# A graph aggregation inside a fused block: boundary chunks gathered once for two groups, and groups dealt anew over the stages

## The chip, the cores and the metric

The kernel runs on one NeuronCore of a Trainium2 chip. Its engines work side by side, each through its own queue in order, and wait for one another by semaphores: TensorE (PE, matmuls; its weight loads are listed apart as PEld), VectorE (DVE), ScalarE (ACT), GpSimd (POOL, which here issues the gathers) and SyncE (SP, which issues the other transfers). The metric is the device time of one execution in microseconds (us). Time before: a median of 1892.01 us of three runs (1885.59 to 1893.51).

## The reference, cut to what matters

A block over 6250 rows of 512: a layer norm, then a graph branch and an attention branch added to x, and a feed-forward branch at the end. The part that the change touches is the graph branch's sum over 100,000 edges:

```python
h = jax.nn.relu(x @ W1 + b1) @ W2 + b2
row, col = (edge_index[0], edge_index[1])      # src, dst
agg = jax.ops.segment_sum(h[col], row, num_segments=h.shape[0])
return h + agg
```

The attention branch (keys, queries, values, a projection, an MLP with a GELU) and the feed-forward branch are dense products; they matter here as the work between which the sum is done.

## The kernel before, in words

**Tiling.** The rows are 50 tiles of P=125 rows. Two tiles make a step, so each dense stage is a loop of STEPS=25 steps. The stages follow one another on the time line: a first pass over x that makes the keys and the rows r = relu(x W1 + b1) and stores r as the table `hidden_rows` (to 449 us of the profile), the turn (449 to 510 us), the second pass with values and queries (`phase2`, 510 to 1105 us), the MLP (1105 to 1585 us), and the tail with the sums' product and the feed-forward branch (to 1872 us). Since the product with W2 is linear, the edges are summed over r and multiplied afterwards.

**Edges.** During the first pass DVE sorts the 100,000 edges by the tile and row that they add to; PE transposes blocks of keys between. The sorted list is cut into chunks of 128 edges, and two neighbouring chunks make a unit of 256. A unit on the boundary between two tiles has edges of both. A *group* is one unit seen from one tile: there are PAIRS = 390 + 50 = 440 groups. `rank_part` (DVE) and `sort_part` (PE) work out, in the last steps of the first pass, which unit and tile each of the 440 groups has; the tiles with the fewest edges come first.

**A group** costs work on four engines. POOL issues two gathers of 128 rows each (L650), one for either chunk, into a ring of RING=12 groups. ACT makes, in batches of BP=4 groups, the one-hot matrices that say which row of the tile each edge adds to: eight activations (L1334) and one over all of them (L1338), into two buffers by turns, so batch q waits until the groups of batch q-2 are done. PE multiplies one-hots by gathered rows, four half-precision products (L912, twice L913, L915; the rows lie as high and low halves), into the banks BE and BH by turns. DVE adds the bank to the tile's sums in `acc` (L1826). Group n on PE waits for its gathers, its batch and the addition of group n-2.

**The order** is written by hand. `TURN`, `SECOND`, `BETWEEN`, `MLP`, `JOIN` and `LAST` say how many groups stand in each stretch: 4 ahead of the product that makes `kptv` (L1002) and 4 behind the one that makes `pmat` (L1014), 8 in each step of `phase2`, 8 between, 6 in each MLP step, 6 in the join, and the remaining 68 over 21 of the tail's steps. In a step of `phase2` the eight places are: behind the value product of either tile (L951 to L953), then behind the query product (L768 to L770) and the folded product (L755 to L757) of the next step's first tile, the same for its second tile, and behind each half of the output product (L985). I call them v0, v1, q0, w0, q1, w1, y0 and y1.

ACT's batches have fixed places: one behind the exponentials (L1252) of a step and one behind the copy of the transposed queries (L1372) and the cast of the next x (L1262), each a batch ahead of need. In the tail a batch stands ahead of `scaled_rows` (L1416), on which the next tail step's products (L1113, L1145) wait. `fetch_sums` on SP waits until `pairs_of_smallest(u)` groups are added.

## Time and profile before

| what | value |
|---|---|
| median of 3 runs | 1892.01 us (1885.59 to 1893.51) |
| the profiled execution, its own time | 1874.1 us |
| its span, first to last instruction | 1872.3 us |
| PE busy | 1596.6 us (85%) |
| DVE busy | 1135.9 us (61%) |
| ACT busy | 823.8 us (44%) |
| POOL busy | 1038.9 us (55%), of it 866.4 us in 880 gather issues |
| mean granted TensorE clock | 0.95 |

The profiled execution is 17.9 us shorter than the median; sums below are made on its time line and then set on the median. A timeline row gives the start, the length, the engine, the line and, in square brackets, how long the engine stood idle before it and what ended that. A matmul's length overlaps the next one's, so the spacing of starts tells what a matmul costs. The granted clock of 0.5 is the 1.2 GHz level of TensorE and 1.0 the 2.4 GHz one.

### The profile page before, as it was taken

What the parts mean: (1) busy time and instruction counts of PE and PEld (TensorE: products, weight loads), DVE (VectorE), ACT (ScalarE), POOL (GpSimd) and SP (SyncE); (2) the same over time, 40 slices, a digit from 0 to 9 for tenths busy, and PEclk for the clock granted to TensorE, in tenths of its full rate; (3) what the DMA queues carried; (4) which work ended last, traced back from release to release, by engine and by line L of the source; (5) the groups of instructions that cost most, each with busy time, mean ns of one, the idle gap of its engine ahead of it and who ended that gap; (6) DMA issues with size and microseconds to landing.
All of it is one profiled execution on the core that took longest, in us unless ns stands there. A gap on an engine that the chain in (4) does not pass through costs nothing.

```text
span 1872.3 us, 26899 instructions
## 1 busy us (share of the span) xinstructions
PE 1596.6 (85%) x8883; PEld 1260.8 (67%) x8883; DVE 1135.9 (61%) x2520; ACT 823.8 (44%) x1896; POOL 1038.9 (55%) x1107
## 2 busy tenths in 40 slices
PE   5999999988788998989889867888888887689886
PEld 4778878776566776666666646777767766466664
DVE  5899998984144455444444445554555554487785
ACT  2144444444043333434334354555455554355562
POOL 3024434335466666666666666566766665477630
PEclk8999999998899999999999988999999998799997
DMA  6023322223245455555555464555555554566652
GB/s 182 22 73 116 94 88 89 81 84 116 59 146 184 146 153 156 155 160 158 156 155 156 138 194 147 161 172 179 175 175 175 178 172 141 152 212 217 204 181 71
DMA packets 91083, 270.21 MB, mean 144 GB/s; under 512 B 19355, under 2 KB 21403, under 8 KB 90946
## 3 DMA queue, kind: packets, MB, share of 16 engines
q1 hardware_dynamic: 47490, 149.05, 23.9%
q0 software_dynamic: 43456, 119.44, 22.9%
q8 instruction: 73, 1.20, 0.3%
q14 instruction: 64, 0.52, 0.1%
HBM read 217.19 MB, written 44.90 MB: 140 GB/s over the span
## 4 chain that ended last, share of the span: by engine, by line
PE 50%; DVE 16%; issue 15%; ACT 7%; DMA 6%; another core or an unknown queue 3%; POOL 3%; DVEq 0%; SPq 0%; POOLq 0%; ACTq 0%
DVE sb_weights L1523 6%; PE bank L985 4%; PE bank L951 3%; PE bank L952 2%; PE bank L953 2%; ACT sb_weights L1334 2%; DMA sb_step<-y_rows 2%; PE turn_bank L913 2%; PE bank L1052 2%; PE bank L913 2%; PE bank L756 2%; PE bank L757 2%; PE bank L1054 2%; PE bank L1053 2%
## 5 line engine op out<-in xcount | busy, mean ns | idle before, releaser
L650 POOL DMA_INDIRECT sb_weights<-hidden_rows,sb_weights x880 | 866.4, 985 | 461.2 <-issue 227.0
L1334 ACT ACTIVATE sb_weights<-sb_const,sb_weights 128x125 f16<-128x125 f16 x880 | 266.9, 390 | 73.4 <-remote 31.3
L1826 DVE TENSOR_TENSOR sb_acc<-sb_acc,bank 125x257 f32 x220 | 92.5, 421 | 237.9 <-remote 107.6
L1826 DVE TENSOR_TENSOR sb_acc<-sb_acc,turn_bank 125x257 f32 x220 | 92.4, 420 | 202.6 <-remote 109.2
L1252 ACT ACTIVATE sb_step<-sb_step 125x256 f32<-125x256 f32 x100 | 50.3, 507 | 264.6 <-DVE sb_step L1696 261.6
L1523 DVE TENSOR_TENSOR sb_weights<-sb_weights 128x512 f32<-128x512 f32 (+3 forms) x256 | 164.4, 684 | 3.6
L755 PE MATMUL bank<-sb_w_parts,sb_x_high 128*125 128x512 f32 (+1 forms) x400 | 139.9, 350 | 3.5 <-issue 3.5
L617 POOL TENSOR_SCALAR sb_const<-sb_const 125x2 f32<-125x2 f32 x25 | 10.2, 410 | 238.5 <-ACT sb_step L1236 238.5
L1372 ACT COPY sb_step<-bank 128x500 f32<-128x500 f32 x25 | 14.4, 577 | 289.4 <-remote 229.2
L757 PE MATMUL bank<-sb_w_parts,sb_x_low 128*125 128x512 f32 (+1 forms) x400 | 135.8, 340 | 3.8 <-issue 3.4
L756 PE MATMUL bank<-sb_w_parts,sb_x_high 128*125 128x512 f32 (+1 forms) x400 | 136.0, 340 | 2.0 <-issue 1.8
L1338 ACT ACTIVATE sb_weights<-sb_weights,sb_const 128x1000 f16<-128x1000 f16 x110 | 124.2, 1129 | 3.6
L768 PE MATMUL bank<-sb_w_parts,sb_x_high 128*125 128x256 f32 (+1 forms) x300 | 103.0, 343 | 15.3 <-DVE sb_step L1704 12.7
L1052 PE MATMUL bank<-sb_mlp_high,sb_gelus_high 128*125 128x512 f32 x200 | 85.9, 430 | 29.3 <-issue 20.7
L985 PE MATMUL bank<-sb_const,sb_step 128*125 128x512 f32 x200 | 101.7, 633 | 2.1 <-issue 1.9
L912 PE MATMUL turn_bank<-sb_weights 128*125 128x257 f16 x220 | 62.7, 285 | 43.9 <-issue 40.5
L912 PE MATMUL bank<-sb_weights 128*125 128x257 f16 x220 | 62.4, 284 | 40.2 <-issue 20.6
L1358 ACT ACTIVATE sb_step<-sb_step,sb_const 125x512 f32<-125x512 f32 x50 | 37.9, 805 | 133.4 <-DMA sb_step<-y_rows 123.0
L770 PE MATMUL bank<-sb_w_parts,sb_x_low 128*125 128x256 f32 (+1 forms) x300 | 95.0, 317 | 0.0
L769 PE MATMUL bank<-sb_w_parts,sb_x_high 128*125 128x256 f32 (+1 forms) x300 | 95.0, 317 | 0.0
L913 PE MATMUL turn_bank<-sb_weights 128*125 128x256 f16 x440 | 87.3, 279 | 5.4 <-issue 5.4
L868 PE MATMUL bank<-sb_step 125*128 125x256 f32 x400 | 90.8, 380 | 1.1 <-ACT sb_step L1312 1.1
(361 smaller groups left out, 4312.5 us busy)
## 6 DMA issues: line engine op xcount, KB each, us to landing
sb_step<-x SPq DMA_DIRECT2D x63, 500.0 KB
sb_step<-x_t SPq DMA_DIRECT2D x50, 500.0 KB
sb_weights<-hidden_rows,sb_weights POOLq DMA_INDIRECT x880
y_rows<-sb_step SPq DMA_DIRECT2D x25, 500.0 KB
sb_step<-y_rows SPq DMA_DIRECT2D x25, 500.0 KB
z_rows<-sb_step SPq DMA_DIRECT2D x25, 500.0 KB
sb_step<-z_rows SPq DMA_DIRECT2D x13, 504.0 KB
out<-sb_step SPq DMA_DIRECT2D x13, 500.0 KB
```

The source lines that it names most:

```text
L650: pool.indirect_dma_start(out=ring[:, n % RING * 2 + h, 0:HID], out_offset=None, in_=table, in_offset=bass.IndirectOffsetOnAxis(ap=row_of[ ...
L755: pe.matmul(bk, high, rhs(0, c), start=c == 0, stop=False)
L756: pe.matmul(bk, high, rhs(1, c), start=False, stop=False)
L757: mm = pe.matmul(bk, low, rhs(0, c), start=False, stop=c == KC - 1)
L912: pe.matmul(bk[0:P, 0:RW], one_hot, row[:, LOW_AND_ONE], start=True, stop=False)
L913: mm = pe.matmul(bk[0:P, 0:HID], one_hot, row[:, HIGH], start=False, stop=False)
L985: mm = pe.matmul(banks[m][0:P, :], qpT[:, c, m * P:(m + 1) * P], pmat[:, c, :], start=False, stop=c == KH - 1)
L1052: pe.matmul((BC, BD)[m][0:P, :], high, w_high, start=k == 0, stop=False)
L1334: mm = act.activation(hit[q % 2][:, i, :], iota_h[:, :], ACT.Abs, bias=less_lane[:, q * BP + i // 2, i % 2:i % 2 + 1])
L1338: act.activation(hit[q % 2], hit[q % 2], ACT.Relu, scale=-1.0, bias=one_c[:, 0:1]).then_inc(hits, 1)
L1523: sort_op(dve.tensor_tensor(half(target, c, lo), a, b, op))
L1826: dve.tensor_tensor(dst, dst, (BE, BH)[n % 2][0:P, 0:RW], ALU.add).then_inc(g_add, 1)
```

## The change

A boundary unit of a *step's two tiles* (tile 2k and tile 2k+1) is now gathered once, and two groups in a row read it: the tile before the boundary and the tile behind it. There are 25 of those. These 50 groups come first, in the order of the tiles' sizes; the other 390 follow. The ring holds units, so 12 slots may cover up to 24 groups. UNITS = 440 - 25 = 415, and POOL issues 830 gathers instead of 880. PE, ACT and DVE still have 440 groups, 110 batches and 440 additions. The index work in `rank_part` gets two more small columns and loses `begun`.

The counts become TURN = (6, 14, 16): 6 ahead of the `kptv` product, 14 between the query products of step 0 and the `pmat` product, and 16 behind that one; SECOND = 14, 10, 9, 8 and then 7 for each of 21 steps (188 instead of 200); LAST = 52 instead of 68; BETWEEN, MLP and JOIN stay. ACT makes batches by need (`hits_until`) instead of at two fixed places of each step.

```diff
-TURN, SECOND, BETWEEN, MLP, JOIN = 8, [8] * STEPS, 8, [6] * STEPS, 6
-BEFORE_MLP = TURN + sum(SECOND) + BETWEEN
+TURN, SECOND, BETWEEN, MLP, JOIN = (6, 14, 16), [14, 10, 9, 8] + [7] * (STEPS - 4), 8, [6] * STEPS, 6
+BEFORE_SECOND = [sum(TURN) + sum(SECOND[:u]) for u in range(STEPS + 1)]
+BEFORE_MLP = BEFORE_SECOND[STEPS] + BETWEEN
...
-    return PAIRS * (2 * u + 2) // NT
+    return NT + (PAIRS - NT) * (u + 1) // STEPS
+def unit_of(n):
+    return n // 2 if n < NT else n - STEPS
...
-                for n in range(issued[0], min(end, PAIRS)):
-                    if n == 0:
+                for r in range(issued[0], min(end, UNITS)):
+                    if r == 0:
                         pool.wait_ge(k_mm, STEPS * 2 + 1)
-                    if n >= RING:
-                        pool.wait_ge(g_mm, n - RING + 2)
+                    if r >= RING:
+                        pool.wait_ge(g_mm, last_pair(r - RING) + 2)
...
-                    pe.wait_ge(gathered[n % RING], 32 * (n // RING + 1))
+                    r = unit_of(n)
+                    pe.wait_ge(gathered[r % RING], 32 * (r // RING + 1))
...
-            groups(TURN // 2)
+            groups(TURN[0])
             pe.wait_ge(*made("hk"))
...
                 qw_product(Step(2, 0), m)
+            groups(TURN[1])
             pe.wait_ge(*made("kptv"))
...
-            groups(TURN - TURN // 2)
+            groups(TURN[2])
             pe.wait_ge(*made("pmat"))
...
             one_hots(0)
+            one_hots(1)
             act.copy(w2_halves[0][:, 0:V_AT].bitcast(F32R), raw_q[:, 0:V_AT]).then_inc(ev("q_high"), 1)
...
                 exps(t, lambda t: act.wait_ge(qn, t.u + 1))
-                one_hots(2 * t.u + 3)
+                hits_until(BEFORE_SECOND[t.u])
...
-                one_hots(2 * t.u + 4)
+                hits_until(BEFORE_SECOND[t.u] + sum(spread(SECOND[t.u], 8)[0:4]))
             for u in (0, 1):
                 high_parts(Step(2, u), k_mm, STEPS * 2)
-            one_hots(1)
-            one_hots(2)
+            hits_until(sum(TURN[:2]))
...
             q_rows(Step(2, 0))
+            add_groups(TURN[1])
             dve.wait_ge(ev("pe_pmat"), 1)
```

Line numbers of the changed kernel are 21 to 24 higher from here on. On PE in the turn, where the folded product of step 0's second tile (L755 to L757) ends and the `pmat` product (L1014) stands, before:

```order
L757 MATMUL bank<-sb_w_parts,sb_x_low 125x256
L1014 MATMUL bank<-sb_step 128x512 x8
L912 MATMUL bank<-sb_weights 125x257
L913 MATMUL bank<-sb_weights 125x256 x2
L915 MATMUL bank<-sb_weights 125x257
L912 MATMUL turn_bank<-sb_weights 125x257
```

and now (L934, L935 and L937 are a group, L1037 is the `pmat` product):

```order
L937 MATMUL bank<-sb_weights 125x257
L934 MATMUL turn_bank<-sb_weights 125x257
L935 MATMUL turn_bank<-sb_weights 125x256 x2
L937 MATMUL turn_bank<-sb_weights 125x257
L1037 MATMUL bank<-sb_step 128x512 x8
L934 MATMUL bank<-sb_weights 125x257
```

Fourteen groups now stand between the folded product and `pmat`, and sixteen behind it.

On ACT at the same place, from the cast of the query weights (`sb_w_parts`, 128x2304) to the exponentials (L1252) of step 0, before:

```order
L1344 CAST sb_w_parts<-sb_weights 128x2304
L1262 CAST sb_x_high<-sb_step 128x1000 x2
L1334 ACTIVATE sb_weights<-sb_const,sb_weights 128x125 x8
L1338 ACTIVATE sb_weights<-sb_weights,sb_const 128x1000
L1334 ACTIVATE sb_weights<-sb_const,sb_weights 128x125 x8
L1338 ACTIVATE sb_weights<-sb_weights,sb_const 128x1000
L1252 ACTIVATE sb_step<-sb_step 125x256 x2
```

and now (L1357 and L1361 are a batch, L1275 the exponentials):

```order
L1368 CAST sb_w_parts<-sb_weights 128x2304
L1285 CAST sb_x_high<-sb_step 128x1000 x2
L1357 ACTIVATE sb_weights<-sb_const,sb_weights 128x125 x8
L1361 ACTIVATE sb_weights<-sb_weights,sb_const 128x1000
L1357 ACTIVATE sb_weights<-sb_const,sb_weights 128x125 x8
L1361 ACTIVATE sb_weights<-sb_weights,sb_const 128x1000
L1357 ACTIVATE sb_weights<-sb_const,sb_weights 128x125 x8
L1361 ACTIVATE sb_weights<-sb_weights,sb_const 128x1000
L1357 ACTIVATE sb_weights<-sb_const,sb_weights 128x125 x8
L1361 ACTIVATE sb_weights<-sb_weights,sb_const 128x1000
L1357 ACTIVATE sb_weights<-sb_const,sb_weights 128x125 x8
L1361 ACTIVATE sb_weights<-sb_weights,sb_const 128x1000
```

Five batches, not two, stand between the casts and the exponentials, and four more follow ahead of the copy of the transposed queries.

On ACT in the tail, two neighbouring steps between the rows of L1402 and L1416, before:

```order
L1402 COPY sb_step<-bank 1x250
L1334 ACTIVATE sb_weights<-sb_const,sb_weights 128x125 x8
L1338 ACTIVATE sb_weights<-sb_weights,sb_const 128x1000
L1416 ACTIVATE sb_step<-bank,sb_step 125x512 x2
```

and now a step that has no batch (L1425 is the copy, L1439 the scaled rows):

```order
L1431 ACTIVATE sb_step<-bank,sb_const 128x125 x2
L1425 COPY sb_step<-bank 1x250
L1439 ACTIVATE sb_step<-bank,sb_step 125x512 x2
L1421 COPY sb_step<-bank 128x250
L1416 CAST sb_w_parts<-bank 128x500
```

Of the tail's batches behind step 0 there were 15, and 11 are left.

## Rows read from the trace of the kernel before

**Rows 1.** The page: busy time, share of the span, and number of instructions.
```profile
PE 1596.6 (85%) x8883; PEld 1260.8 (67%) x8883; DVE 1135.9 (61%) x2520; ACT 823.8 (44%) x1896; POOL 1038.9 (55%) x1107
```
**Rows 2.** Table: stretch, length, busy PE, PEld, DVE, ACT, POOL, clock, DMA share, GB/s.
```profile
449.00:510.00 61.00, 43.04 (x169) 29.81 (x170) 13.94 (x23) 7.38 (x18) 31.29 (x33) 0.77 0.26 76
...
534.00:1106.00 572.00, 504.42 (x2800) 387.54 (x2800) 284.80 (x791) 228.46 (x529) 372.42 (x385) 0.97 0.53 156
...
1630.00:1865.00 235.00, 202.74 (x1078) 150.31 (x1078) 180.73 (x462) 125.67 (x299) 126.61 (x133) 0.97 0.55 179
```
**Rows 3.** Timeline of PE in the turn.
```profile
453.88 0.44 PE L912 MATMUL bank<-sb_weights 128*125 128x257 f16 x1 [5.25 <-DMA sb_weights<-hidden_rows,sb_weights]
...
457.05 0.48 PE L912 MATMUL bank<-sb_weights 128*125 128x257 f16 x1 [0.32 <-issue]
...
458.82 4.47 PE L1002 MATMUL bank<-sb_step,sb_w_parts 128*128 128x256 f32 x16
...
499.27 7.03 PE L1014 MATMUL bank<-sb_step 128*128 128x512 f32 x16
506.14 0.27 PE L912 MATMUL bank<-sb_weights 128*125 128x257 f16 x1
...
506.58 0.27 PE L912 MATMUL turn_bank<-sb_weights 128*125 128x257 f16 x1
...
508.86 0.29 PE L912 MATMUL bank<-sb_weights 128*125 128x257 f16 x1 [1.68 <-DVE sb_acc L1826]
...
509.86 0.48 PE L951 MATMUL bank<-sb_w_parts,sb_x_high 128*125 128x512 f32 x1
```
**Rows 4.** Timeline of POOL in the turn.
```profile
448.28 0.94 POOL L650 DMA_INDIRECT sb_weights<-hidden_rows,sb_weights  x1 [0.30 <-issue]
449.53 0.95 POOL L650 DMA_INDIRECT sb_weights<-hidden_rows,sb_weights  x1 [0.30 <-issue]
...
507.01 0.94 POOL L650 DMA_INDIRECT sb_weights<-hidden_rows,sb_weights  x1 [20.28 <-PE bank L915]
```
**Rows 5.** Timeline of DVE in the turn: query rows, then the additions behind `pmat`.
```profile
500.54 0.48 DVE L1696 SCALAR_TENSOR_TENSOR sb_step<-bank,sb_const 125x256 f32<-125x256 f32 x1
506.34 1.29 DVE L1871 COPY sb_const<-bank 128x512 f32<-128x512 f32 x2 [5.32 <-PE bank L1014]
508.29 0.42 DVE L1826 TENSOR_TENSOR sb_acc<-sb_acc,bank 125x257 f32 x1 [0.66 <-issue]
508.91 0.42 DVE L1826 TENSOR_TENSOR sb_acc<-sb_acc,turn_bank 125x257 f32 x1 [0.20 <-DVE sb_acc L1826]
```
**Rows 6.** Timeline of PE from w1 to the end of a step of `phase2`.
```profile
573.47 0.27 PE L912 MATMUL turn_bank<-sb_weights 128*125 128x257 f16 x1
...
577.80 0.29 PE L912 MATMUL bank<-sb_weights 128*125 128x257 f16 x1 [2.02 <-issue]
...
581.37 0.29 PE L912 MATMUL turn_bank<-sb_weights 128*125 128x257 f16 x1 [1.23 <-issue]
```
**Rows 7.** Timeline of ACT in the same step: the second batch.
```profile
575.93 2.42 ACT L1334 ACTIVATE sb_weights<-sb_const,sb_weights 128x125 f16<-128x125 f16 x8
578.38 1.13 ACT L1338 ACTIVATE sb_weights<-sb_weights,sb_const 128x1000 f16<-128x1000 f16 x1
```
**Rows 8.** Timeline of ACT and PE in the tail: a step with a batch, then one without.
```profile
1682.65 1.12 PE L1113 MATMUL bank<-sb_weights,sb_step 126*125 126x512 f32 x2 [0.95 <-ACT sb_step L1416]
...
1692.46 1.12 PE L1113 MATMUL bank<-sb_weights,sb_step 126*125 126x512 f32 x2 [0.95 <-ACT sb_weights L1416]
...
1701.15 1.02 PE L1113 MATMUL bank<-sb_step 126*125 126x512 f32 x2
```
**Rows 9.** Timeline of PE in the tail: another pair, without a batch and then with one.
```profile
1755.32 1.16 PE L1145 MATMUL bank<-sb_step 128*128 128x125 f32 x8 [0.94 <-issue]
...
1764.19 1.05 PE L1145 MATMUL bank<-sb_step 128*128 128x125 f32 x8
...
1775.23 0.94 PE L1145 MATMUL bank<-sb_step 128*128 128x125 f32 x7
```

More of the change, by code:

```diff
@@ L662, in _ @@
             for a in range(STEPS):
-                gathers(BEFORE_MLP + sum(MLP[:a]) + RING)
-            gathers(BEFORE_LAST - JOIN + RING)
+                gathers(units_before(BEFORE_MLP + sum(MLP[:a])) + RING)
+            gathers(units_before(BEFORE_LAST - JOIN) + RING)
             roots(steps[0])
             for b in range(STEPS - 1):
-                gathers(BEFORE_LAST + sum(LAST[:b]) + RING)
+                gathers(units_before(BEFORE_LAST + sum(LAST[:b])) + RING)
                 roots(steps[b + 1])
-            gathers(PAIRS)
+            gathers(UNITS)
         @block.tensor
@@ L909, in groups @@
                     for h in (0, 1):
-                        bk, one_hot, row = (BE, BH)[n % 2], hit[n // BP % 2][:, n % BP * 2 + h, :], ring_h[:, n % RING * 2 + h]
+                        bk, one_hot, row = (BE, BH)[n % 2], hit[n // BP % 2][:, n % BP * 2 + h, :], ring_h[:, r % RING * 2 + h]
                         if h == 0:
@@ L1730, in rank_part @@
                     dve.wait_ge(ev("pe_ends"), 1)
-                    size, counted, place, first, last, shift = (rank_cols[0:NT, i:i + 1] for i in range(6))
-                    count_row, ranked = BG[0:NT, 8:8 + NT], iota_p[0:NT, 0:NT]
-                    dve.scalar_tensor_tensor(out=size, in0=BG[0:NT, 2:3], scalar=64.0, in1=after_tile[0:NT, :], op0=ALU.mult, op1=ALU.add)
+                    size, counted, place, first, last, shift, shared, taken = (rank_cols[0:NT, i:i + 1] for i in range(8))
+                    count_row, ranked, odd_tile = BG[0:NT, 8:8 + NT], iota_p[0:NT, 0:NT], after_tile[0:NT, 1:2]
+                    in_order, pure = past[0:NT, 0:NT], past[0:NT, NT:PAIRS]
+                    dve.scalar_tensor_tensor(out=size, in0=BG[0:NT, 2:3], scalar=64.0, in1=after_tile[0:NT, 0:1], op0=ALU.mult, op1=ALU.add)
                     seq(dve.scalar_tensor_tensor(out=size_row[0:NT, :], in0=BG[0:NT, 64:64 + NT], scalar=64.0, in1=ranked, op0=ALU.mult, op1=ALU.add))
@@ L1744, in rank_part @@
+                    dve.tensor_scalar(tile_cols[0:NT, :], ones[0:NT, :], after_tile[0:NT, 0:1], None, ALU.mult)
+                    seq(dve.tensor_scalar(in_order, iota_p[0:NT, 1:NT + 1], place, None, ALU.is_equal))
+                    dve.scalar_tensor_tensor(out=shared, in0=BG[0:NT, 0:1], scalar=1.0, in1=taken, op0=ALU.add, op1=ALU.subtract)
                     dve.tensor_scalar(shift_cols[0:NT, :], ones[0:NT, :], shift, None, ALU.mult)
                     dve.wait_ge(iota_in, 16)
-                    seq(dve.tensor_scalar(begun[0:NT, :], iota_g[0:NT, :], 1.0, first, ALU.add, ALU.is_ge))
@@ L1747, in rank_part @@
-                    seq(dve.scalar_tensor_tensor(out=past[0:NT, :], in0=iota_g[0:NT, :], scalar=last, in1=begun[0:NT, :],
+                    seq(dve.tensor_scalar(pure, iota_g[0:NT, NT:PAIRS], first, None, ALU.is_ge))
+                    dve.tensor_scalar(shared_cols[0:NT, :], ones[0:NT, :], shared, None, ALU.mult)
+                    seq(dve.scalar_tensor_tensor(out=pure, in0=iota_g[0:NT, NT:PAIRS], scalar=last, in1=pure,
                                                  op0=ALU.is_lt, op1=ALU.mult))
```

49 lines of the change are left out of this document (27 added, 22 removed).

## The prediction

> **What bounds the kernel now.** I read the page's busy shares first, then the table by stretch, then the timelines of the places where groups are added or taken away. PE is busy 85% of the span and POOL 55% [rows 1], so a gather saved is worth nothing by itself: what counts is how long PE needs from one place to the next. In the 24 steps of `phase2` between 534 and 1106 us PE is busy for 504.42 of 572 us, and in the tail for 202.74 of 235 [rows 2]. The rest are waits of PE for DVE and ACT, not for gathers: POOL is busy for only 372.42 of the 572 us and 126.61 of the 235 [rows 2]. In the turn PE waits 5.25 us for the first gathered rows [rows 3]; afterwards the ring is full so early that POOL itself stands idle for 20.28 us until PE frees a slot [rows 4]. The change therefore moves PE's, ACT's and DVE's work more than it removes anything. The question is what a group costs where it goes and what it gave where it was.
>
> **Gathers, 50 fewer.** POOL's issues follow 1.25 us apart (448.28 and 449.53 [rows 4]), so a unit takes 2.5 us and 25 saved units 62 us of POOL. The cover is PE's own pace. Price: 0. The few index instructions in `rank_part` and `sort_part` change by two or three small ones: 0.
>
> **The turn, first part: two more groups ahead of `kptv`.** They read units that are on their way anyway: the third unit lands before 457.05 us, when the third group, which read it before, could start [rows 3]. All six can then follow at PE's pace here, and end about when four did: +0.4 us (458.82 becomes 459.2 [rows 3]).
>
> **The turn, fourteen groups ahead of `pmat`.** The place is 499.27 us [rows 3]. Two limits apply. DVE and PE hand the two banks to and fro: additions follow 0.62 us apart (508.29, 508.91 [rows 5]), 0.65 with the signal. ACT needs 3.6 us for a batch of four (575.93 to 578.38 + 1.13 [rows 7]), 0.9 us a group, and may start batch q only when batch q-2 is used up. Walking it through: groups 6 to 11 have their batches (1 and 2) ready; DVE is free at 501.0 [rows 5]; they end at 503.9. Batch 3 could start when group 7 ended, 500.2, so it is there at 503.8, and groups 12 to 15 end at 506.4. Batch 4 is there at 507.5, and groups 16 to 19 end at 510.2. So `pmat` begins 10.9 us later.
>
> **The turn, sixteen groups behind `pmat`.** `pmat` takes 6.87 us (499.27 to 506.14 [rows 3]) and ends at 517.1. Groups 20 and 21 go at once; the next waits for DVE, whose copy of `pmat` delays the first addition by 1.95 us (506.34 to 508.29 [rows 5]) as before. Batches 5 and 6 were made beside `pmat`, so groups up to 27 end at 523.5. Batch 7 is started when group 23 is done, 520.9, and there at 524.5; batch 8 at 528.1. Groups 28 to 31 end at 527.1 and 32 to 35 at 530.7. With the 0.4 us, `phase2` begins at 531.1 instead of 509.86 [rows 3]: **+21 us** for 28 groups, 0.76 us each. If ACT held nothing up, DVE's 0.65 us would give 17 to 18.
>
> **Steps 0 to 3 of `phase2`** get 6, 2, 1 and 0 groups more. A group in a full stretch of PE costs 0.44 us (506.14 to 506.58 [rows 3]): 9 x 0.44 = +4.0 us. Their batches come late, too. The batch that stands behind the copy of the transposed queries is ready at 579.5 in the step I looked at (578.38 + 1.13 [rows 7]). Before, no group of its own step read it. In steps 0 and 1 now the group at w1 does, to which PE comes at 573.47 [rows 6]: 6.0 us of waiting, in place of the 2.02 and 1.23 us that PE waits in this step behind it for DVE [rows 6], so 2.8 us net, twice: +5.6 (0 if the waits behind absorb all of it, 12 if none).
>
> **Steps 4 to 24** each have seven groups instead of eight; the one at v0 goes. 21 x 0.44 = **-9.2 us**. The idle time of the stretch is 572 - 504.42 = 67.6 us [rows 2], 0.35 us for each of its 192 groups; if all of it went with the groups, one would be worth 0.79 us and the term -16.6. I take 0.44, since the waits in rows 6 stand at y0 and y1, which stay. In five steps (6, 10, 14, 18, 22, where three groups of a batch are gone at the step's start) the group at y0 needs the late batch: 579.5 against 577.80 [rows 6, 7], +1.7 us, of which the wait of 1.23 us behind it gives back most: 5 x 0.5 = +2.4. The MLP and the stretch between have the same counts at the same place in a batch: 0.
>
> **The tail** has 16 groups and 4 batches fewer. A batch is dear here, because it stands ahead of the scaled rows for which PE waits. A step with a batch takes 1692.46 - 1682.65 = 9.81 us, the next without one 1701.15 - 1692.46 = 8.69 [rows 8]; another pair gives 8.87 without and 11.04 with [rows 9]. The differences are 1.1 and 2.2; I take 1.6: 4 x 1.6 = **-6.4 us**. In steps that wait for the batch anyway a group fewer gives nothing, so of 16 x 0.44 = 7.0 us I count **-5**. The ends are -4.5 in all (1.1 a batch, groups nothing) and -15 (16 groups at 0.44 + 0.5, the tail's 32.3 us of idle over its 64 groups, the batches in it).
>
> **The sum:** 0.4 + 20.8 + 4.0 + 5.6 - 9.2 + 2.4 - 5.0 - 6.4 = **+12.6 us**, on the profiled execution's own 1874.1 us 1886.7, and on the median 1904.6. I round to **1904**, 0.6% slower.
>
> **Rival 1, the other side: the waits belong to the groups.** If PE's idle time in `phase2` and the tail comes with each group (a bank not yet added, a batch not yet made) and not with each step, groups taken out give 0.79 us there and 0.94 in the tail. Then: turn +17.5 (DVE's pace), steps 0 to 3 +7.1, steps 4 to 24 -16.6, tail -15, late batches 0: **-7 us, 1885**. For it: the two waits in a `phase2` step [rows 6] are both ahead of a group. Against it: they stand at y0 and y1, where the number of groups stays. It decides from about 0.7 us a group. Were stretches of the turn also bound less than I think (15 us), it would reach -10, faster by the bound below.
>
> **Rival 2: the clock in the turn.** Thirty groups with waits between them leave PE busy for 0.44 of about 0.8 us. In the turn PE's granted clock is already 0.77 on average [rows 2], and behind the 5.25 us wait a product takes 0.44 us that takes 0.27 later, the 1.2 GHz level [rows 3]. If it falls again between 499 and 531 us, groups go from 0.76 to about 0.9 us, `pmat` from 6.9 to 13.8, and the first products of step 0 pay some us: +10 more, **1914**. A wait of 1.68 us among the groups behind `pmat` did not bring it down (0.29 us a product [rows 3]). The Trainium skill (TensorE: Matmul & The Clock Gate, "HAM oscillation — how this bites in real kernels") says that bursts of matmuls broken by waits can send the array back to its slow clock, over and over; by that rule the sum would be +22 instead of +12.6. The row on the first group agrees with it for one long wait; no row here shows it for short ones.
>
> **Rival 3: the change starves the ring.** Thirty groups in 31 us read 15 units, which POOL's 2.5 us a unit would just deliver; the ring begins full, and 15 units (12, and 3 for the slots of the first six groups) are issued by 483 us, 30 issues from 445.8, two before the 448.28 of rows 4, so a landing would have to be late by ten us or more to bind. Price if it did: some 5 us, 1909, within the forecast's range.
>
> **How the numbers follow.** A measurement of this kernel can tell about 0.5% (9.5 us) from no change; "faster" is below 1882.5 and "slower" above 1901.5. The forecast, with its ends (1896 to 1911, rival 3 in it), has 0.50; rival 2 0.12; rival 1 0.38, nearly half of it beyond 9.5 us, since both its bounds may lie too near. The forecast lies close above 1901.5, so a part (0.13) of its weight is "same"; rival 1 gives 0.2 to "same" and 0.18 to "faster". So: faster 0.18, same 0.33, slower 0.49. The range that leaves out a tenth on each side is 1879 to 1917.
>
> **What would show it.** In the new profile: `phase2` begins at about 531 us, with waits of PE for ACT or DVE of 1 to 1.5 us between fours of groups; POOL's long idle stretch in the turn stays; steps 0 and 1 have a wait for a batch at w1 of some us; steps 4 to 24 are 0.4 us shorter on average (0.8 for rival 1); the tail is 11 us shorter. The prediction is wrong if the turn grows by less than 17 us, if steps 4 to 24 give back over 15, or if the clock in the turn falls to 0.5 for over 10 us more than now.

## The result, and the profile after

The changed kernel takes 1867.38 us, median of four runs (1851.62 to 1873.57), the kernel before 1892.76 (1885.59 to 1894.26): a ratio of 0.9868, interval [0.9836, 0.99]. A second comparison on another chip gave 0.9924 [0.9903, 0.9944], a third with single runs 0.988. It is faster by 0.8 to 1.3%; 0.6% slower was forecast. In one comparison, and in that one alone, the kernel before took 1761.75 us (a single run) where its medians in the others were 1872 to 1893, on a chip that gave 1872 at another time; it is told where it is used.

The profiled execution took 1851.62 us. PE's work is that of before, POOL has 50 gathers less. First the page's busy line and its row of the gathers, then the table by stretch, to be read beside [rows 1, 2].

```profile
PE 1592.7 (86%) x8883; PEld 1268.0 (69%) x8883; DVE 1134.7 (61%) x2523; ACT 828.3 (45%) x1896; POOL 995.6 (54%) x1057
...
L671 POOL DMA_INDIRECT sb_weights<-hidden_rows,sb_weights x830 | 823.0, 992 | 476.7 <-issue 210.4
```

```profile
449.00:532.00 83.00, 60.98 (x281) 44.31 (x282) 24.47 (x49) 31.63 (x78) 54.32 (x55) 0.81 0.31 91
556.00:1087.00 531.00, 485.57 (x2724) 380.73 (x2723) 272.22 (x771) 212.83 (x489) 333.57 (x345) 0.96 0.52 157
1611.00:1842.00 231.00, 201.40 (x1054) 149.87 (x1052) 178.31 (x455) 113.78 (x265) 102.10 (x109) 0.97 0.51 167
```

The second stretch is the 24 steps of `phase2` behind the first. It is 531 us long instead of 572, and PE's idle time in it is 45.4 us instead of 67.6: more is gone than the own products of the 18 groups fewer that these steps have (PE's busy time fell by 18.9 us).

Where the time went, stage by stage (us). The stages are cut at the same instructions in each kernel: the first product for `kptv`, the first of `phase2`, DVE's last row operation of step 3 and of step 24, DVE's last of the MLP and of the tail. "Again" is a second pair of profiles, of one chip.

| stage | before | after | after less before | forecast | again |
|---|---|---|---|---|---|
| turn, `kptv` to `phase2` | 51.0 | 72.9 | +21.9 | +21.2 | +38.7 |
| steps 0 to 3 | 97.2 | 105.0 | +7.8 | +9.6 | +3.2 |
| steps 4 to 24 | 498.3 | 450.9 | **-47.4** | -6.8 | -59.1 |
| MLP | 479.8 | 488.6 | +8.8 | 0 | +9.7 |
| tail | 279.6 | 266.0 | -13.6 | -11.4 | -14.5 |

One stage decides. A step with eight groups takes 23.7 us, one with seven 21.5 on average; 14 of the 21 take between 20.9 and 21.1. A group taken out, with its two gathers, gives 2.3 us, where 0.44 was said and 0.79 was the other end.

### The profile page after: what moved, and what is told of

Same layout as the page of the kernel before. It is cut to its first block, busy times and chain, and to the rows that moved or that the text cites. A ratio compares the mean times of both kernels' runs of the same rounds, so it can differ in the third digit from the quotient of the medians.

```text
span 1849.4 us, 26852 instructions
## 1 busy us (share of the span) xinstructions
PE 1592.7 (86%) x8883; PEld 1268.0 (69%) x8883; DVE 1134.7 (61%) x2523; ACT 828.3 (45%) x1896; POOL 995.6 (54%) x1057
## 4 chain that ended last, share of the span: by engine, by line
PE 49%; DVE 17%; issue 12%; ACT 8%; DMA 5%; another core or an unknown queue 5%; POOL 2%; SPq 1%; DVEq 1%; POOLq 0%; ACTq 0%
DVE sb_weights L1546 6%; PE bank L1007 4%; ACT sb_weights L1357 3%; PE bank L973 2%; PE bank L975 2%; PE bank L974 2%; PE bank L1075 2%; PE bank L935 2%; PE bank L1077 2%; PE turn_bank L935 2%; DMA sb_step<-sb_acc 2%; PE bank L1076 2%; PE bank L1066 2%; PE bank L1065 2%
## 5 line engine op out<-in xcount | busy, mean ns | idle before, releaser
L671 POOL DMA_INDIRECT sb_weights<-hidden_rows,sb_weights x830 | 823.0, 992 | 476.7 <-issue 210.4
L1357 ACT ACTIVATE sb_weights<-sb_const,sb_weights 128x125 f16<-128x125 f16 x880 | 266.4, 388 | 88.2 <-PE turn_bank L937 53.8
L1853 DVE TENSOR_TENSOR sb_acc<-sb_acc,turn_bank 125x257 f32 x220 | 92.5, 421 | 227.1 <-PE turn_bank L937 81.1
L1853 DVE TENSOR_TENSOR sb_acc<-sb_acc,bank 125x257 f32 x220 | 92.4, 420 | 226.0 <-remote 69.2
L1275 ACT ACTIVATE sb_step<-sb_step 125x256 f32<-125x256 f32 x100 | 50.4, 507 | 250.1 <-DVE sb_step L1719 240.2
L1361 ACT ACTIVATE sb_weights<-sb_weights,sb_const 128x1000 f16<-128x1000 f16 x110 | 124.2, 1129 | 3.7
L934 PE MATMUL bank<-sb_weights 128*125 128x257 f16 x220 | 64.3, 292 | 52.5 <-issue 20.6
L1075 PE MATMUL bank<-sb_mlp_high,sb_gelus_high 128*125 128x512 f32 x200 | 87.2, 436 | 25.2 <-DVE sb_gelus_low L2046 11.3
L934 PE MATMUL turn_bank<-sb_weights 128*125 128x257 f16 x220 | 64.1, 291 | 44.0 <-issue 31.2
L935 PE MATMUL turn_bank<-sb_weights 128*125 128x256 f16 x440 | 89.4, 285 | 2.1 <-issue 2.1
L935 PE MATMUL bank<-sb_weights 128*125 128x256 f16 x440 | 88.7, 284 | 1.9 <-issue 1.8
```

The costliest lines, as they stand in the source:

```text
L671: pool.indirect_dma_start(out=ring[:, r % RING * 2 + h, 0:HID], out_offset=None, in_=table, in_offset=bass.IndirectOffsetOnAxis(ap=row_of[ ...
L934: pe.matmul(bk[0:P, 0:RW], one_hot, row[:, LOW_AND_ONE], start=True, stop=False)
L935: mm = pe.matmul(bk[0:P, 0:HID], one_hot, row[:, HIGH], start=False, stop=False)
L1075: pe.matmul((BC, BD)[m][0:P, :], high, w_high, start=k == 0, stop=False)
L1357: mm = act.activation(hit[q % 2][:, i, :], iota_h[:, :], ACT.Abs, bias=less_lane[:, q * BP + i // 2, i % 2:i % 2 + 1])
L1361: act.activation(hit[q % 2], hit[q % 2], ACT.Relu, scale=-1.0, bias=one_c[:, 0:1]).then_inc(hits, 1)
```

## A signal that comes late

Why the eighth group costs so much shows in no total. (The addition is L1826 in the kernel before and L1853 in the changed one, the last product of a group L915 and L937.) This is the timeline of the kernel before at one place in a step: the last product of a group on PE, then the addition on DVE and the gather on POOL, both of which wait for that group.

```profile
976.90 0.27 PE L915 MATMUL turn_bank<-sb_weights 128*125 128x257 f16 x1
977.23 0.95 POOL L650 DMA_INDIRECT sb_weights<-hidden_rows,sb_weights  x1 [0.30 <-issue]
978.48 0.95 POOL L650 DMA_INDIRECT sb_weights<-hidden_rows,sb_weights  x1 [0.30 <-issue]
...
979.73 0.94 POOL L650 DMA_INDIRECT sb_weights<-hidden_rows,sb_weights  x1 [0.30 <-issue]
...
980.00 0.28 PE L755 MATMUL bank<-sb_w_parts,sb_x_high 128*125 128x256 f32 x1
980.58 0.28 PE L756 MATMUL bank<-sb_w_parts,sb_x_high 128*125 128x256 f32 x1 [0.30 <-issue]
...
981.28 0.28 PE L757 MATMUL bank<-sb_w_parts,sb_x_low 128*125 128x256 f32 x1
981.99 0.38 PE L755 MATMUL bank<-sb_w_parts,sb_x_high 128*125 128x256 f32 x1 [0.43 <-issue]
982.08 0.58 ACT L1372 COPY sb_step<-bank 128x500 f32<-128x500 f32 x1 [11.79 <-remote]
982.11 0.42 DVE L1826 TENSOR_TENSOR sb_acc<-sb_acc,turn_bank 125x257 f32 x1 [5.25 <-remote]
982.25 0.94 POOL L650 DMA_INDIRECT sb_weights<-hidden_rows,sb_weights  x1 [1.58 <-remote]
```

The group ends at 977.18 us by PE's record. DVE has been idle for 5.25 us when it starts the addition at 982.11, and POOL starts 0.14 us behind it. Two engines that wait for one signal start together, 4.9 us late. "remote" means that the profile finds no instruction to which it could put the release. PE then waits for additions at y0 and y1 [rows 6]; those waits had been read as belonging to the step.

ACT starts at the same moment (982.08), though it waits for other products of PE, the transposes (L973), which end at 977.61 by the record. And PE itself stands still there: its folded product (L755 to L757) waits for no semaphore and normally starts a part every 0.12 us, but from 980.00 on single parts start 0.58 and 0.7 us apart, until 981.99. In steps 4 to 24 such holes inside products add up to 11.3 us in this profile of the kernel before, and none stands in the changed kernel's or in that of half the gathers. So more is held up at this place than one signal.

The same place in a kernel with half the gathers (experiment 3):

```profile
896.94 0.27 PE L937 MATMUL turn_bank<-sb_weights 128*125 128x257 f16 x1
...
897.35 0.42 DVE L1853 TENSOR_TENSOR sb_acc<-sb_acc,turn_bank 125x257 f32 x1 [1.43 <-PE turn_bank L937]
897.49 0.94 POOL L671 DMA_INDIRECT sb_weights<-hidden_rows,sb_weights  x1 [1.85 <-PE turn_bank L937]
```

Here the two follow 0.14 and 0.28 us behind the recorded end (897.21). The Trainium skill (Perfetto Trace Analysis, "Summary: the profiler window per engine type") says that the end shown for a TensorE instruction is an estimate and that the way of its signal is not in the profile; the 0.14 and the 4.9 us behind ends that look alike agree with that. So the profile can't tell a signal that travels late from work of PE that ends later than its record; "late signal" below stands for either.

The view of waits on DVE, over steps 4 to 24, adds them up (us in total, times, longest). The kernel before:

```profile
DVE sb_acc L1826 <- remote: 100.5, 30, 6.1
DVE sb_acc L1826 <- PE turn_bank L915: 57.3, 26, 5.4
DVE sb_acc L1826 <- PE bank L915: 42.3, 20, 4.6
```

The changed kernel, and the kernel with half the gathers:

```profile
DVE sb_acc L1853 <- PE bank L937: 87.8, 30, 5.4
DVE sb_acc L1853 <- PE turn_bank L937: 83.6, 30, 5.4
```

```profile
DVE sb_acc L1853 <- PE bank L937: 68.0, 38, 2.9
DVE sb_acc L1853 <- PE turn_bank L937: 44.1, 30, 2.8
```

In the changed kernel the "remote" row has shrunk from 100.5 to 2.6 us, but single waits are still up to 5.4 us; with half the gathers none is over 2.9.

When is a signal late? For every addition of an execution, from start to end, that waited over 0.5 us I took the distance from PE's recorded end to its start, and asked whether POOL was inside a gather for at least half of the microsecond around that end:

| kernel | POOL gathering: additions, mean | POOL pausing: additions, mean |
|---|---|---|
| before (three profiles) | 136 to 145, 3.0 to 3.3 us | 23 to 28, 0.5 to 0.6 us |
| after (three profiles) | 138 to 140, 2.1 to 2.3 us | 43 to 46, 0.5 to 0.7 us |

Over the whole execution signals are late where POOL gathers and prompt where it pauses. Two limits go with the table. The distance also holds time in which DVE did other work; DVE's idle time just before these additions is 2.2 to 2.3 us on average in the kernel before, 1.6 in the changed one. And in steps 4 to 24 alone the two kernels differ more than the two columns: 2.9 to 3.3 us in the kernel before while POOL gathers, only 1.2 to 1.3 us in the changed kernel, against 0.8 to 1.0 us there while POOL pauses. With seven units a step most of the lateness is gone also beside a gather.

POOL needs 1.25 us a gather, so 20 us for eight units and 17.5 for seven. A step in which no signal is late takes 20.06 us (experiment 3): eight units fill it, seven leave 2.5 us of pause. That last sentence is a reading and not shown: in fact POOL waits about as long in both kernels over steps 4 to 24 (90 and 92 us), in the kernel before because the step has grown to 23.7 us. All this is an association; the runs below change the gathers to see whether they are the cause.

## The experiments

Two theories stood first. A: dealing the groups anew pays (fewer in the steps of `phase2`). B: gathering less pays. In each kernel below everything not named is as in the changed kernel.

**1. Shared gathers, old counts.**

```diff
-TURN, SECOND, BETWEEN, MLP, JOIN = (6, 14, 16), [14, 10, 9, 8] + [7] * (STEPS - 4), 8, [6] * STEPS, 6
+TURN, SECOND, BETWEEN, MLP, JOIN = (4, 0, 4), [8] * STEPS, 8, [6] * STEPS, 6
```

> One part alone: the 25 boundary units are gathered once (830 gathers), but the groups are dealt as before: TURN 4 and 4, SECOND 8 in each step, 68 in the tail. Theory A (what pays is the dealing, and above all seven groups instead of eight in a step of the second pass: a step fell from 23.7 to 21.0 us for one group less): the same time as the kernel before, ratio 0.997 to 1.003, steps still 23 to 24 us. Theory B (what pays is fewer gathers): faster, ratio 0.99 or less.

1844.27 us, ratio 0.9847 [0.98, 0.9894]. The 50 gathers alone give all of the gain. By the profiles 17 of the 32 us come where most of them are left out: steps 0 to 3, whose groups share units, take 79.9 us instead of 97.2. The turn, whose eight groups share too, took 41.8 us, in the profiles of the kernel before 46 to 51. Steps 4 to 24, with a unit for nearly each group, take 23.70 us each as before. Theory A is not needed for the gain.

**2. New counts, every group its own unit.**

```diff
-UNITS = PAIRS - STEPS
+UNITS = PAIRS
 def unit_of(n):
-    return n // 2 if n < NT else n - STEPS
+    return n
```

> The other part alone: every one of the 440 groups has gathers of its own (880), but the groups are dealt as in the changed kernel. Theory A: the steps of the second pass keep their 21.0 us; the turn gets longer, since 36 groups need 36 units at 2.5 us each and the ring holds 12, by 10 to 30 us; in sum 0 to 20 us slower than the changed kernel. Theory B: steps go back towards 23.7 us and the time to that of the kernel before or worse.

1913.48 us, ratio 1.0207 [1.0171, 1.0242]: slower. The turn takes 120.0 us and steps 0 to 3 122.9; steps 4 to 24 take 21.18 us each and the tail 264.1, as after. It is 37 us slower than before. The two parts don't add: sharing is worth 25 to 32 us with the old counts (three comparisons) and some 50 with the new ones (1913.5 against the 1856 to 1867 of the changed kernel on other chips). The 28 groups put into the turn fetch a unit each in this kernel, and the ring runs dry: from 506.32 us to the end of the turn at 582.15 POOL pauses for under 10 us beyond its 1.25 us a gather. The prediction's sum doesn't describe this kernel, since its rival 3 counted on 15 units for the turn's 30 groups; nor does the run price the new dealing by itself, with gathers in time. With shared units on one chip (single runs, experiment 6) old counts took 1860.06 us and new ones 1866.38. That steps 4 to 24 take 21.18 us with seven units of their own, as in the changed kernel, does carry over.

**3. Eight groups a step, and half the gathers.**

```diff
-[14, 10, 9, 8] + [7] * (STEPS - 4)
+[14, 10, 9, 8] + [8] * (STEPS - 4)
```

> The changed kernel with eight groups in steps 4 to 24 of the second pass instead of seven (21 groups more there, 31 in the tail instead of 52). Theory A1 (the eighth group itself costs over 2 us, because with it a step falls into the slower pattern): these steps take 23 to 24 us, and the second pass gets 45 to 60 us longer. Theory A2 (the changed places of ACT's batches, not the number of groups, made the steps short): they take 21.5 us, 0.44 more than with seven. The tail gets shorter by 8 to 15 us in both.

1891.86 us, ratio 1.0099 [1.0061, 1.0136]; 23.83 us a step against 21.47. The eighth group with its two gathers costs 2.4 us.

```diff
-    return n // 2 if n < NT else n - STEPS
+    return n // 2
```

> The groups are dealt as before, but every gathered unit is used for two groups, so that there are 440 gathers instead of 880 (the sums are then not the reference's). It halves the traffic and the issues of the gathers in every stage. Theory B (gathers slow the other engines down, by memory traffic or by POOL): the steps of the second pass fall from 23.7 to 22 us or less. Theory A: they stay at 23 to 24 us, and the time within 0.5% of the kernel before.

With the old counts and all 220 units shared (so that the sums are no longer the reference's): 1708.65 us, ratio 0.9116 [0.9084, 0.9148]. Steps with **eight** groups take 20.06 us. So most of the 2.4 us is not the group's own (its products, addition, batch): eight groups with eight gathers fit into less time than seven with fourteen (20.9 to 21.1 us). A slot of the ring covers two groups here; the kernel with one wide gather a group, below, has no such reach and takes 20.09 us too, so that isn't it. 440 gathers fewer save 168 us, 0.38 us each; the MLP falls from 18.16 to 16.62 us a step (steps 1 to 24), the tail by 7 us.

**4. What of a gather costs: the instruction or the bytes?** Beside each of the 440 gathers a narrow one:

```diff
+                        pool.indirect_dma_start(
+                            out=spare[:, r % RING * 2 + h, :], out_offset=None, in_=table.rearrange("n (a b) -> (n a) b", b=4),
...
+                    pe.wait_ge(gathered[r % RING], 64 * (r // RING + 1))
```

> The kernel with the groups dealt as before and all 220 units shared (440 gathers, the sums not the reference's), which took 1708 us and 20.06 us per step of phase2, plus beside each gather a second, narrow one: 125 rows of 16 B instead of 1 KB, to a place that is not read; PE waits for it too. So there are as many gather instructions as before (880), and half of the bytes. Theory B1 (what a gather costs is its issue, its descriptors and signals): the step goes back to about 23.7 us, the MLP to 18.2, the whole to about 1875 us. Theory B2 (what it costs is the bytes that it moves): the step stays at 20.1 to 20.6 us, the whole at 1710 to 1730. Before, DVE's additions that waited started 2.9 us behind PE's recorded end on average, with half the gathers 0.84: B1 says about 2.9, B2 about 0.9.

And one gather of 2 KB rows in place of a group's two (`hidden_rows` is stored twice, side by side, for it):

```diff
-                    for h in (0, 1):
-                        pool.indirect_dma_start(
-                            out=ring[:, r % RING * 2 + h, 0:HID], out_offset=None, in_=table,
+                    pool.indirect_dma_start(
+                        out=slots[:, r % RING * 2 * RW:r % RING * 2 * RW + 2 * HID], out_offset=None, in_=table,
```

> The opposite: groups dealt as before, every group its own unit, but one gather of 2 KB rows in place of two gathers of 1 KB rows (the hidden rows are stored twice side by side in phase 1, so that 2 KB are there to be read; the sums are not the reference's). 440 gather instructions with the bytes of before's 880. B1: about 20.1 us per step of phase2 and 16.6 in the MLP, as with half the gathers; the whole some 1720 us (the doubled stores lie beside phase 1). B2: 23.7 us per step, 18.2 in the MLP, the whole about 1875 us.

1734.23 and 1770.7 us, 20.05 and 20.08 us a step: neither the count nor the bytes seemed to cost anything. But the kernel before took 1761.75 us beside them. In that comparison gathers were cheap for every kernel, and nothing could be told apart. So both went again, with the two given kernels, on the same chip at another time.

> The kernel before itself, unchanged, so that its profile stands beside those of the next three kernels on one chip. On the chip of the runs with 440 narrow or wide gathers it took 1761.75 us, on the two chips before 1877 and 1892 us. Theory C (what a gather costs belongs to the chip and its state: signals that come late): on a quick chip its phase2 steps take 20.2 to 20.8 us and the waiting additions start under 1 us behind PE's recorded end, on a slow chip 23.7 us and 2.9 us. Theory B1 (own gathers always cost 2.4 us a step or more): 23 us or more on either.

> The kernel with 440 wide and 440 narrow gathers (the sums not the reference's), once more beside the kernel before with a profile of that. If this chip is a slow one (before about 1880 us): B1 (count) gives 23.7 us per phase2 step and some 1875 us, B2 (bytes) 20.1 us and some 1730. If it is a quick one: 20.05 us per step and about 1734 us, as measured.

> The kernel with 440 gathers of 2 KB rows in place of 880 of 1 KB (the sums not the reference's), once more. If this chip is a slow one: B1 (count) gives 20.1 us per phase2 step and some 1770 us in all, B2 (bytes) 23.7 us and some 1880. If it is a quick one: 20.1 us per step, 19.0 in the MLP and about 1771 us, as measured.

Before: 1873.07 us, ratio 1.0017 to itself, 24.03 us a step. Narrow gathers added: **1932.53**, ratio 1.0326 [1.0273, 1.0379], 23.63 us a step. One wide gather: **1769.81**, ratio 0.9457 [0.9434, 0.948], 20.09 us a step. In `phase2` all the bytes in half the instructions cost nothing, and half the bytes in all the instructions cost as much as before: there it is the number of gather instructions, not what they move. (The 60 us that the narrow kernel takes more than the kernel before stand in the turn, 78.1 against 46.2 us, and the tail, 305.5 against 279.6.) An instruction also asks for 128 rows of any width, and the rows halve with the instructions; these runs don't part the two. Nor is it the packets that the gathers' queue moves: from 600 to 1000 us 12,789 in the kernel before, 12,756 in the wide one, 10,618 in the narrow one.

The MLP is another matter. A step there takes 18.16 us before, 16.62 with half the gathers, 17.96 with narrow ones added and 18.82 with wide ones. So the wide kernel, quick in `phase2`, gives nothing back in the MLP, and of the 61 us between it (1769.81) and the kernel with half the gathers (1708.65) the MLP has 58. Whether that is the bytes isn't shown: from 1100 to 1400 us ACT waits 139.4 us for the loads of y in the wide kernel, 125.1 with half the gathers.

DVE's waits in steps 4 to 24 say the same. Narrow gathers added, in the first comparison and in the second:

```profile
DVE sb_acc L1858 <- PE bank L942: 75.6, 42, 2.2
DVE sb_acc L1858 <- PE turn_bank L942: 37.8, 30, 2.8
```

```profile
DVE sb_acc L1858 <- remote: 125.2, 24, 7.1
DVE sb_acc L1858 <- PE turn_bank L942: 67.3, 33, 3.0
```

One wide gather, in the second:

```profile
DVE sb_acc L1853 <- PE bank L937: 78.9, 42, 2.2
DVE sb_acc L1853 <- PE turn_bank L937: 38.5, 34, 2.8
```

The narrow pair is one kernel on one chip. Its additions start 0.62 us behind PE's recorded end while POOL gathers in the one profile, 3.02 us in the other; while POOL pauses, 0.46 and 0.34 us. POOL is equally busy in both (322 and 320 us in steps 4 to 24), 965 to 998 ns a gather. So a run of gathers is needed for late signals and does not suffice: there is a state of the device in which they are late (in five of the six comparisons here) and one in which they are not, dear and cheap in what follows; theory C in the expectations says just this. The cheap one stood in a single comparison of single runs, without a profile of the kernel before. The kernel with 440 wide gathers took about the same in both, 1770.7 and 1769.8 us; in the cheap comparison it was slower than the kernel before.

**5. POOL's time, and other traffic.** Behind each of 440 gathers three small operations in a chain, and, apart from that, three copies of 512 KB a step on SP's queue:

```diff
+                        for _ in range(3):
+                            pool_seq(pool.tensor_tensor(pool_tiny[0:P, :], neg_one[0:P, :], neg_half[0:P, :], ALU.pow))
```

```diff
+                for k in range(3):
+                    sp.dma_start(scrap[k][:, u * 2:u * 2 + 2, :], x_d[:, u % STEPS * 2:u % STEPS * 2 + 2, :]).then_inc(scrapped, 16)
```

> 440 gathers (the sums not the reference's) and behind each gather three small operations on POOL, one waiting for the other, so that POOL is about as busy as before without more gathers. Theory B3 (POOL's time is what binds: a slot that comes free waits for POOL): the step goes back to 23 us or more, the whole to 1840 to 1880 us. B1 and B2: the step stays near 20.1 us, the whole at 1708 to 1720 us.

> 440 gathers (the sums not the reference's), and in each step of phase2 and of the MLP SP issues three copies of 512 KB from memory to memory, 1.5 MB a step where the gathers left out moved 1.05 MB; nothing waits for them before the end. If any traffic beside PE's work costs what the gathers cost (a form of B2), the step goes to 23 us or more and the whole to over 1850 us. If only gathers do it, the step stays at 20.1 to 20.8 us and the whole at 1708 to 1740 us.

2229.43 and 2088.6 us, and neither tells what it was made for. With the copies a step of steps 4 to 24 took 23.76 us, the number that the first forecast gave, but not by its cause: the additions that waited started 0.13 to 0.25 us behind PE's recorded end there. The chained operations made POOL's round for a unit longer than PE's for two groups, so PE starved (29.69 us a step); the table from 650 to 1200 us shows POOL at 87% and PE at 75%:

```profile
650.00:1200.00 550.00, 412.97 (x2175) 328.81 (x2173) 223.37 (x623) 181.83 (x420) 477.74 (x597) 0.89 0.29 87
```

The copies stood in SP's queue ahead of the loads of x, and ACT waited for those (waits from 650 to 900 us):

```profile
ACT sb_x_high L1294 <- DMA sb_step<-x_t: 64.0, 11, 12.5
```

Both ran in the comparison in which gathers were cheap, too. What they do show is what a starved ring or a full load queue looks like: a wait put down to one's own DMA or POOL, not additions that start late.

**6. The two given kernels once more.**

> The changed kernel itself, unchanged, beside the kernel before on this chip. Theory C: on a quick chip there is nothing for the seventh or eighth gather to slow, a group less in a phase2 step gives back about its own 0.44 to 0.8 us (9 to 17 us in steps 4 to 24) and the turn costs about 21 us, so the ratio is about 1.00 to 1.01, near what was predicted; on a slow chip 0.985 as before. Theory B1: 0.985 to 0.99 on either.

1856.16 us, ratio 0.9924 [0.9903, 0.9944], beside experiment 4's second comparison. Dear again, so the forecast for the cheap state (ratio about 1.00) was not tried; the 0.985 said for the dear one was missed by 0.7 points.

> The kernel before, unchanged, once more with a profile. It has taken 1761.75 us in one comparison and 1872 us in another on the same chip, so the gathers' price is a matter of a state (call it dear or cheap). Theory C: in the cheap state its phase2 steps take 20.2 to 20.8 us and additions that waited start under 1 us behind PE's recorded end; in the dear state 23.7 to 24.0 us and 2.9 us. Theory B1 alone (own gathers cost 2.4 us a step or more always): never below 23 us, whatever the whole takes.

> The changed kernel beside it. In the cheap state theory C expects what the prediction's sum said, since nothing slows the eighth group: turn about 21 us longer, steps 4 to 24 shorter by 9 to 17 us only, tail 11 us shorter, so 1765 to 1775 us against 1762. In the dear state 1850 to 1865 us against 1865 to 1880.

> The first 25 units shared, the groups dealt as before. Cheap state: 50 gathers fewer beside work that hides them are worth nothing or little, 1752 to 1764 us. Dear state: 1840 to 1850 us.

1890.61, 1866.38 and 1860.06 us, one run each on a third chip: again dear. What the changed kernel does where gathers are cheap stays open; the state could not be called up.

**7. Seven groups a step without the long turn.** If seven units a step are what pays, the 21 groups could go into the tail:

```diff
-TURN, SECOND = (6, 14, 16), [14, 10, 9, 8] + [7] * (STEPS - 4)
+TURN, SECOND = (4, 0, 4), [8] * 4 + [7] * (STEPS - 4)
```

> The first 25 units shared; the turn and steps 0 to 3 of phase2 with their old counts, steps 4 to 24 with seven groups, and the 21 groups that this leaves over in the tail (89 groups there instead of 68). If a step of phase2 with seven own units takes 21.0 us instead of 23.7 in the dear state (as in the changed kernel) and a group in the tail costs 0.85 us, steps 4 to 24 give back some 50 us and the tail takes 18 more: 1812 to 1822 us, faster than both. If the tail is bound by POOL (4.2 units a step at 2.5 us), it takes up to 35 us more: 1830. Cheap state: a group in the tail costs more than it gave in phase2, 1760 to 1775 us.

1874.88 us, one run, where 1812 to 1822 or, with the tail bound by POOL, 1830 was said. Steps 4 to 24 gave back 48 us against experiment 1 on that chip (451.3 against 499.0), and the tail took 52 more (334.1 against 281.9): 2.5 us a group, what POOL needs for a unit. Of 200 us in the tail POOL is in an instruction for 142, and its issues take most of the rest:

```profile
1600.00:1800.00 200.00, 160.51 (x817) 118.87 (x815) 127.56 (x326) 106.28 (x258) 142.03 (x146) 0.91 0.64 187
...
POOL sb_weights L671 <- issue: 33.1, 112, 0.3
```

So the groups belong in the turn, but fewer of them than the change puts there: (6, 10, 12) there, eight in each of steps 0 to 3, 69 left for the tail.

> A version that may beat both kernels: the first 25 units shared, 28 groups in the turn (6, 10, 12), eight in each of steps 0 to 3 of phase2, seven in steps 4 to 24, 69 groups left for the tail. From the stages measured in the dear state: against the kernel with shared units and old counts, 20 groups more in the turn cost 1.1 us each (+22), steps 0 to 3 lose some of their shared units (+5), steps 4 to 24 give back 47 to 50 us, the tail stays: 20 to 25 us faster than that kernel, ratio to the kernel before 0.970 to 0.976. If POOL's pauses, not the count of groups, decide (the turn takes units that steps 0 to 3 then fetch without a pause), the gain shrinks: 0.980 to 0.987, no better than the changed kernel. Cheap state: 1.00 to 1.01.

> The first 25 units shared, the groups dealt as before, beside the other version and the kernel before on one chip. Dear state: 0.982 to 0.988 of the kernel before, as in the two comparisons so far (0.985 both). Cheap state: 0.993 to 1.002.

1839.84 us, ratio **0.9838** [0.9816, 0.986], and for shared gathers with the old counts on the same chip 1848.46, 0.9878 [0.9858, 0.9898]. The turn took 68.2 us against 42.0, steps 4 to 24 446.4 against 497.1, the MLP 491.4 against 471.4. The gain of the first is 9 us, not the 20 to 25 expected; its ratio lies in the range that the expectation gave for the case that POOL's pauses decide. By the profiles the turn took 26 us for 20 groups and the MLP, whose counts are the same, 20 us more; but the profiled execution of the second (1834.54 us) is 14 us under its median, so these differences are rough. It is the lowest ratio of the kernels whose sums are the reference's (experiment 1 gave 0.9847 on another chip, inside the interval), and it beats the kernel before surely; against the changed kernel (0.9868 and 0.9924 on other chips) it was not run side by side.

## Why the prediction was wrong, step by step

**Gathers, 50 fewer: the step that failed.** "The cover is PE's own pace. Price: 0." POOL's time is covered, that much held; but a gather costs time beside PE's work, and experiment 1 and its two repetitions put 25 to 32 us on the 50 left out. The runs show this price; that it comes by way of PE's late signals is the reading of the traces above. The prediction asked only whether a gather ends in time, never what it does to others while it runs.

**Steps 4 to 24: the same failure in another term.** The mechanism (a group costs its four products) was sized from a row in a stretch where POOL was idle for 20.28 us [rows 4]. The other end, 0.79 us, shared out PE's idle time evenly. Measured: 2.3 to 2.8 us, of which the group's own part is small, since eight groups with half the gathers take 20.06 us. The prediction's own sign of being wrong, steps 4 to 24 giving back over 15 us, came with 47. The waits at y0 and y1 [rows 6] were called the step's own. The first was for an addition that DVE had been idle 5.36 us for, the second for one that stood behind it in DVE's order; the rows named no releaser but "issue", which should have been a reason to look at DVE:

```profile
577.24 0.42 DVE L1826 TENSOR_TENSOR sb_acc<-sb_acc,bank 125x257 f32 x1 [5.36 <-remote]
```

**The turn: right by luck.** `phase2` was to begin at 531.1 and began at 531.43. On the way little held.

```profile
503.46 8.08 PE L1037 MATMUL bank<-sb_step 128*128 128x512 f32 x16
...
524.89 0.29 PE L934 MATMUL bank<-sb_weights 128*125 128x257 f16 x1 [3.18 <-issue]
...
527.04 0.45 PE L934 MATMUL turn_bank<-sb_weights 128*125 128x257 f16 x1 [1.52 <-DVE sb_acc L1853]
...
531.43 0.78 PE L973 MATMUL bank<-sb_w_parts,sb_x_high 128*125 128x512 f32 x1
```

The fourteen groups took 21.1 us (482.4 to 503.46) where 10.9 were said, `pmat` 7.9 instead of 6.87, the sixteen 20.1 instead of 14. What paid for it lay ahead: from the first product for `kptv` to what follows (the fourteen groups now, `pmat` before) it took 23.8 us instead of 40.5. Before, PE waited among those products, in the view of waits from 459 to 509 us:

```profile
PE bank L1002 <- issue: 9.4, 8, 1.7
```

And the granted clock was 0.50 from 477.6 to 494.7 us there. In this execution of the changed kernel no wait stands at that place, and the clock is 1.00 from 458.5 to 482.4 us. In the other profiles of the two kernels the turn grew by 38.7 and 37.2 us. The walk through ACT's batches and DVE's pace gave a floor, not the time. POOL's long idle stretch, which was to stay, is gone: its longest pause in the turn is 4.03 us now. That its gathers make the turn long is likely by the runs on `phase2`, and not shown for the turn.

**Steps 0 to 3:** +7.8, +3.2 and +8.1 for +9.6. The late batch at w1 in steps 0 and 1 is there, two waits of PE for ACT, 5.1 us in all where 5.6 net were said.

**The MLP:** 0 was said, +8.8, +9.7 and +2.6 us measured. The same counts stand at the same places; no run settles what it is.

**The tail:** -13.6, -14.5 and -19.9 for -11.4. Right in two of three.

**Rival 1** (waits belong to the groups, 1885 us, chance 0.38) had the right sign, and its price per group was a third of the measured one. It asked the right question and stopped at a mean. **Rival 2** came in part: the mean clock of the turn is 0.81 against 0.77, but it fell to 0.5 four times between 485 and 532 us, for 10.2, 3.4, 3.4 and 6.9 us, with waits of PE before each. There a group's product takes 0.42 to 0.47 us (the one at 527.04), elsewhere 0.27 to 0.29, also behind the wait of 3.18 us (524.89). The rule of the Trainium skill on oscillation (TensorE: Matmul & The Clock Gate, "HAM oscillation — how this bites in real kernels") agrees with those falls. Of `pmat` it took 1 us (7.9 instead of 6.87), not the 7 of the rival; what it took of the groups no run parts from their waits. **Rival 3** did not come: behind the first group no wait of PE in the turn ends with a gather, though 11.7 us of them have no named releaser.

Against the table: terms that came out within 2.5 us in the profiled pair are the turn, steps 0 to 3 and the tail; steps 4 to 24 missed by 41 us and the MLP by 9. In the other two pairs the turn missed by 16 to 18 us as well. The range ended at 1879, since both its ends were made from the same rows of work, and none from a kernel with other gathers.

## What to carry to other kernels

Work on an engine that is off the critical path, and done in time, can still cost: look whether engines that wait for one signal start together, late, behind a recorded end, and whether that happens while a third engine issues gathers without a pause. Then count such instructions, and not only bytes: a chunk fetched once for two users was worth 1.2 to 1.5% here, half of all gathers 9%, while the new dealing added nothing to it (and cost 2% where every group fetched its own unit and the ring ran dry). And when a piece of work is moved, price it from a stretch with the same company, not from the emptiest one.

## What was not expected of the hardware

- DVE's additions that had waited started 3.0 us behind PE's recorded end on average while POOL gathered, 4.9 us in the place shown, where ACT and POOL started with DVE; 0.14 us behind it where nothing disturbed. Whether the signal or PE's own end is late, the record doesn't tell.
- In `phase2` the price goes with the number of indirect gathers: a step takes 23.6 us with 880 of half the bytes, 24.0 with 880 of all, 20.1 with 440 of all and 20.1 with 440 of half the bytes (another chip). Not so in the MLP. The whole times are 1932.5, 1872, 1769.8 and 1708.7 us.
- It comes and goes with the device: the kernel before took 1761.75 us and 1872 us on the same chip, the one with narrow gathers 1734 and 1932. What sets the state, and what in the chip delays the signal, is open.
